# Segment sums of a graph network by products with masks on TensorE instead of running sums on VectorE

## What is computed

```python
h  = relu(layernorm(x))
m  = segment_sum((h * deg_isqrt)[src] * edge_weight[:, None], dst) * deg_isqrt
x1 = x + leaky_relu((h + m) @ W0.T + b0, 0.01)
y  = relu(layernorm(x1))
for l in range(4):                      # edges and one self loop for each node
    p  = y @ W[l]
    al = leaky_relu((p @ a_s)[src] + (p @ a_d)[dst] + ea @ We[l] @ a_e, 0.2)
    al = segment_softmax(al, dst)
    o  = segment_sum(p[src] * al[:, None], dst) + bias[l]
    y  = layernorm(o) * gamma[l] + beta[l]
out = x1 + y
```

## Time and profile before

| | us |
|---|---|
| median of 3 runs | 3035.37 (3034.85 to 3036.59) |
| profiled execution | 3065.14 |
| its span, first to last instruction | 3063.4 |
| busy: PE / PE weight load | 1802.1 / 1333.8 |
| busy: DVE / ACT / POOL | 1893.5 / 1617.7 / 1276.3 |
| mean granted TensorE clock | 0.731 of full |

### The profile page before, as it was taken

How to read it: one execution, slowest core, us unless ns; L and a number is a source line. 1 busy time by engine, 2 the same in 40 slices (tenths; PEclk the granted TensorE clock), 3 DMA queues, 4 the chain that set the end, 5 groups by cost and what they waited for, 6 DMA issues and landing times. The chain is left out here.

```text
span 3063.4 us, 44584 instructions
## 1 busy us (share of the span) xinstructions
PE 1802.1 (59%) x9650; PEld 1333.8 (44%) x9650; DVE 1893.5 (62%) x9080; ACT 1617.7 (53%) x6973; POOL 1276.3 (42%) x989
## 2 busy tenths in 40 slices
PE   1879999950555659598029496049594068592000
PEld 1756666620333436487026385036484045482000
DVE  3069999941888858234878345968246967114970
ACT  0169999940555759233559354559255567233230
POOL 2668787775111257400037500057400067302277
PEclk9998999975555559579559698559697568796555
DMA  3332233310000341000041100131000131003011
GB/s 104 51 78 65 57 86 96 78 29 1 0 0 1 100 113 34 24 1 1 4 124 31 28 1 1 34 97 34 23 1 1 58 75 43 12 1 84 5 35 36
DMA packets 102065, 126.22 MB, mean 41 GB/s; under 512 B 59950, under 2 KB 67945, under 8 KB 98473
## 3 DMA queue, kind: packets, MB, share of 16 engines
q1 hardware_dynamic: 39016, 97.37, 11.2%
q0 software_dynamic: 62400, 25.68, 5.0%
q10 hardware_dynamic: 432, 0.79, 0.1%
HBM read 78.61 MB, written 64.50 MB: 47 GB/s over the span
## 5 line engine op out<-in xcount | busy, mean ns | idle before, releaser
L241 POOL DMA_INDIRECT S<-row_t,INFG x400 | 528.0, 1320 | 1017.9 <-issue 1017.9
L224 PE MATMUL bank<-ident,Y 125*128 125x125 f32 x1000 | 184.7, 316 | 378.1 <-ACT Y L769 234.6
L754 PE MATMUL bank<-AC,XT 128*125 128x384 f32 x800 | 364.0, 565 | 6.7 <-ACT R L817 6.7
L224 PEld LDWEIGHTS bank<-ident,Y 125*128 125x128 f32 x1000 | 135.3, 164 | 491.6 <-DVE Y L908 228.0
L817 ACT ACTIVATE R<-bank 125x128 f32<-125x128 f32 x1200 | 311.2, 274 | 60.6 <-PE bank L754 60.1
L1517 DVE COPY SCS<-bank 125x8 f32 (+1 forms) x100 | 16.7, 167 | 424.7 <-PE bank L1471 424.7
L1491 ACT ACTIVATE XT<-bank,BC,GC 128x500 f32<-128x500 f32 x150 | 114.3, 762 | 287.0 <-PE bank L224 286.8
L817 ACT ACTIVATION_READ_ACCUMULATOR R<-bank 125x1 f32 x1200 | 247.2, 206 | 0.0
L235 PE MATMUL bank<-WC,XT 128*125 128x128 f32 x1600 | 246.4, 301 | 0.0
L235 PEld LDWEIGHTS bank<-WC,XT 128*125 128x125 f32 x1600 | 206.1, 201 | 49.6 <-issue 49.6
L1089 DVE SCALAR_TENSOR_TENSOR R<-R,keep (+1 forms) x496 | 189.7, 413 | 33.5 <-ACT R L1608 29.4
(11 more groups left out here) (263 smaller groups left out, 5035.4 us busy)
## 6 DMA issues: line engine op xcount, KB each, us to landing
R<-in_x SPq DMA_DIRECT2D x100, 224.0 KB
out_rows<-R SPq DMA_DIRECT2D x100, 224.0 KB
row_t<-T SPq DMA_DIRECT2D x20, 1120.0 KB
S<-row_t,INFG POOLq DMA_INDIRECT x400
R<-in_edge_attr SPq DMA_DIRECT2D x1, 5600.0 KB
x_t<-R SPq DMA_DIRECT2D x5, 1120.0 KB
S<-x_t SPq DMA_DIRECT2D x1, 5600.0 KB
R<-in_x SPq DMA_DIRECT2D x100, 26.0 KB
```

Source lines behind the costliest of these rows:

```text
L224: ins = nc.tensor.transpose(ps[:, a * P:(a + 1) * P], t, ident[0:P, 0:P])
L241: pool.indirect_dma_start(to, None, table, bass.IndirectOffsetOnAxis(ap=idx, axis=0), bounds_check=rows - 1, oob_is_err=False).then_inc(do ...
L754: nc.tensor.matmul(LAYERS[HALVES[a]][0:P, 0:3 * D], h0(g, a), AC[:, 0:3, :], start=True, stop=True).then_inc(layers_done.s, 1)
```

## The change

- The edge order in the tiles is turned: edge e lies in tile e // 125, partition e % 125, so that a tile holds 125 neighbouring edges. Scores and softmax weights stay in the other layout (100 partitions x 125 columns, one tile a partition) and are transposed on PE between the two (`columns_in`, `weights_in`).
- A mask `M` of 125 x 125 in bf16 for each tile, 1 where two edges have the same target, is made once (100 broadcasts of the targets' row by PE, 25 comparisons on DVE) and kept in DRAM (`m_t`, 3.1 MB). It is read back into `R` ahead of the convolution and of each attention layer, since `dense` uses `R`.
- The convolution is one loop of 50 units of two `S` and two `T` tiles (`conv_layer`). For each tile DVE multiplies the mask by the edge weights (`mask`), POOL makes a diagonal for the self term, and PE sums source rows with the mask and the target row with the diagonal in one PSUM tile, ahead of the weights. There are no running sums.
- Attention is one block for the softmax and one loop of 50 units: mask product and diagonal product, copy, product with the layer's weights `WCX`, squares, root, rescale; the next layer's source rows are made beside it. Scores for the next layer come out of the same product as columns 128 and 129 (`W` = 130), so rows of `S`, `T` and `row_t` have 520 bytes. The weights are centred as before, and the preceding layer's gamma is multiplied into them.
- A segment that goes from one tile into the next is summed apart: the first and last column of each aggregated tile is kept (`EDGE`), and behind the loop a 101st tile `T[:, 100]` holds these rows, with steps counted by `x_stage`, `x_pe` and `x_act`.
- In the last layer POOL scatters each unit's tiles in the loop (`put`, lag 5), and x1 rows come in pieces of four tiles (`XF`).
- In `dense` the six dot products are columns 384 to 389 of the product for layers 1 to 3; each tile has a PSUM bank of its own, and ACT copies the six columns to `DOT`.
- Setup: indices are made first, the edge attributes are loaded from setup on (to `T`, row by row of 512 bytes).

The core of the diff:

```diff
-                 # dense, PE: layers(a)
-                                pe.wait_ge(*copied2.at(g + 1))
-                                if g >= 2:
-                                    pe.wait_ge(*mixed2.at(g - 1))
-                                for b in range(Q):
-                                    nc.tensor.matmul(DOTS[g % 2][0:P, b, :], h0(g, b), PC[:, :], start=True,
-                                                     stop=True, skip_group_check=True)
-                            nc.tensor.matmul(LAYERS[HALVES[a]][0:P, 0:3 * D], h0(g, a), AC[:, 0:3, :], start=True,
+                            nc.tensor.matmul(LAYERS[a][0:P, 0:3 * D + 6], h0(g, a), ACB[:, 0:3 * D + 6], start=True,
                                              stop=True).then_inc(layers_done.s, 1)
...
+                            nc.scalar.activation(DOT[:, g % NS, :, a], LAYERS[a][0:P, 3 * D:3 * D + 6], ACT.Copy)
...
+                for g in range(EG):          # DVE, masks
+                    dve.wait_ge(s_rowb, g + 1)
+                    nc.vector.tensor_tensor(M[:, g * Q:(g + 1) * Q, :],
+                                            PT[2 + g % 2][0:P, 0:Q * P].rearrange("p (a e) -> p a e", a=Q),
+                                            DS[:, g * Q:(g + 1) * Q].unsqueeze(2).broadcast_to([P, Q, P]),
+                                            ALU.is_equal).then_inc(s_mask, 1)
...
+                    def aggregate(n):        # convolution, PE
+                        pe.wait_ge(*rows1.at(n + 1))
+                        pe.wait_ge(*masked.at(n + 1))
+                        pe.wait_ge(*diag_ready.at(n + 1))
+                        if n >= NS:
+                            pe.wait_ge(*copied2.at(n - NS + 1))
+                        r = n % NS
+                        for a in range(2):
+                            nc.tensor.transpose(PT[r][:, a * P:(a + 1) * P], Y[:, r, a, :], ident[0:P, 0:P])
+                        for a in range(2):
+                            o = PT[r][:, (2 + a) * P:(3 + a) * P]
+                            nc.tensor.matmul(o, Y[:, r, a, :], MA[:, r, a, :], start=True, stop=False,
+                                             skip_group_check=True)
+                            ins = nc.tensor.matmul(o, Y[:, r, 2 + a, :], DGB[:, r, a, :], start=False, stop=True,
+                                                   skip_group_check=True)
+                        ins.then_inc(gathered.s, 1)
...
+                    for t in slots:          # PE, convolution
+                        run_slot(t, NU, [(4, conv), (7, score), (3, aggregate), (6, turn2)])
+                    for t in slots:          # POOL
+                        run_slot(t, NU, [(2, diagonal), (5, residual), (5, add_beta)])
...
+                dma2(sp, R[:, 0:P * C // 2].bitcast(BF16), m_t, s_ml)    # beside the softmax chain
...
+                    def aggregate(n):        # attention, PE
+                        pe.wait_ge(*masked.at(n + 1))
+                        pe.wait_ge(*diag_ready.at(n + 1))
+                        r = n % NS
+                        if n >= NS:
+                            pe.wait_ge(*t_ready.at(n - NS + 1))
+                        for a in range(2):
+                            o = banks[r][:, a * P:(a + 1) * P]
+                            nc.tensor.matmul(o, S[:, 2 * n + a, 0:D], MA[:, r, a, :], start=True, stop=False,
+                                             skip_group_check=True)
+                            ins = nc.tensor.matmul(o, T[:, 2 * n + a, 0:D], DGB[:, r, a, :], start=False, stop=True,
+                                                   skip_group_check=True)
+                        ins.then_inc(gathered.s, 1)
+                    def multiply(bank, xt, copied, done):
+                        def op(n):
+                            r = n % NS
+                            pe.wait_ge(*copied.at(n + 1))
+                            nc.tensor.matmul(product(banks[bank + r], 2 * P), ones3[:, 0:P],
+                                             BR[:, l:l + 1, 0:cols].broadcast_to([3, 2, cols]), start=True, stop=False,
+                                             skip_group_check=True)
+                            for a in range(2):
+                                ins = nc.tensor.matmul(product(banks[bank + r], 2 * P)[:, a, :],
+                                                       XT[:, r, xt + a * P:xt + (a + 1) * P], WCX[:, l, 0:cols],
+                                                       start=False, stop=True, skip_group_check=True)
+                            ins.then_inc(done.s, 1)
+                        return op
+                    for t in slots:          # PE
+                        run_slot(t, NU, [(0, aggregate), (1, multiply_t)] if final else [(0, turn), (0, aggregate), (1, multiply_t), (0, multiply_s)])
+                    for t in slots:          # ACT
+                        run_slot(t, NU, [(3, root), (1, copy_t), (2, squares)])
+                    def mask(n):             # DVE
+                        r = n % NS
+                        if n >= NS:
+                            dve.wait_ge(*gathered.at(n - NS + 1))
+                        nc.vector.tensor_tensor(MA[:, r, :, :], M[:, 2 * n:2 * n + 2, :],
+                                                alphaS[:, 2 * n:2 * n + 2].unsqueeze(2).broadcast_to([P, 2, P]),
+                                                ALU.mult).then_inc(masked.s, 1)
+                    for t in slots:
+                        run_slot(t, NU, [(0, mask), (4, rescale_t), (3, invert), (1, edge)] if final else [(0, mask), (4, rescale_s), (4, rescale_t), (0, copy_s), (3, invert), (1, edge)])
+                    def put(n):              # POOL, last layer
+                        pool.wait_ge(*t_ready.at(n + 1))
+                        for c in (2 * n, 2 * n + 1):
+                            scatter(pool, out, repNI[:, c:c + 1], N, T[:, c, 0:D], s_out)
+                    for t in slots:
+                        run_slot(t, NU, [(0, diagonal)] + ([(5, put)] if final else []))
```

More of the change, by code:

```diff
@@ L35 @@
 C = E // P
+TC = C + 1
+W = D + 2
 Q = 4
 NS = 4
[L38 to L39 removed]
+NU = C // 2
 GROUPS = N // (P * Q)
@@ new lines, in root @@
+                    def root(n):
+                        r, k = n % NS, 2 if final else Q
+                        act.wait_ge(*squared.at(n + 1))
+                        nc.scalar.activation(rt4[:, r, 0:k], ss4[:, r, 0:k], ACT.Sqrt,
+                                             bias=epsc[:, 0:1]).then_inc(rooted.s, 1)
+                    for t in slots:
+                        run_slot(t, NU, [(3, root), (1, copy_t), (2, squares)])
+                    act.wait_ge(*x_pe.at(3))
+                    nc.scalar.activation(YX[:, :], banks[2][0:C, 0:D], ACT.Square, scale=D ** -0.5,
+                                         accum_out=sx[:, 0:1]).then_inc(x_act.s, 1)
```

1335 lines of the change are left out of this document (697 added, 638 removed).

## The result

The changed kernel takes 2477.36 us (median of 4 runs, 2475.16 to 2483.14) against 3035.98 for the kernel before in the same comparison (median of 4 runs, 3034.85 to 3068.20). The ratio on record, over all these runs, is 0.8143 (95% interval 0.8095 to 0.8190); the two medians alone give 0.816. I had forecast 2682, with 2595 as the lower end.

A forecast was written before the change was run, and what follows sets the result against it. No engine bounds the whole: POOL's transfers end the dense stretches, and attention runs in pieces that hardly overlap. 3063.4 + 37 + 24 - 82 - 79 - 79 - 177 = 2707 us span, 2682 as median; range 2595 to 2830.

The forecast's parts named there:

- Convolution: One loop of 50 units at 6.5 us (5.8 with PE at 2.4 GHz, 7.4 at 1.2): 377 us against 353, +24.
- The lock: Convolution: two-input DVE operations wait for POOL's sums on the shared SBUF port; 0.6 us added to DVE's unit.
- Rival 3: PE at 2.4 GHz also in convolution (-25 to -40) and early block (-45): 2606 us as a median; chance 0.13.
- Layer 1's ramp: Start of layer 1's attention loop: 61 us at half clock kept from the earlier trace, costing 25 us.
- Layers: Layers 2 and 3: chain 24, loop 152, ramp 2, tail 9 make 187 us instead of 266, -79 each.
- Last layer: Scatters overlap the loop from slot 5, POOL sets the unit at 3.9 us: 241 us instead of 418, -177.
- Setup and the next block: Ahead of the dense stretch: setup +15, next block with 100 mask broadcasts +20, one more gather +2; sum +37.
- -5 to -20 case: Block with the mask broadcasts: its cost if PE ran them at 2.4 GHz pace, instead of the +20 forecast.
- POOL's cover: Dense stretches: POOL's queue outlasts compute by 87 us in the first, some 20 in a layer, so added work costs nothing.
- Rival 1: PE stays at 1.2 GHz in the new loops: about 3087 us as a median, slower by 1.7%; chance 0.05.
- rival 2: Clock goes up and down in the loops, attention unit 3.6 us, convolution 7: 2818 us as a median; chance 0.15.
- Rival 4: Last layer: scatters wait for the loop, so overlap fails, 379 us there, 2818 as a median; chance 0.04.

The follow-up runs named there:

- conv_slow4: Changed kernel with four more normalisations per unit of the convolution on ACT; convolution stretch 386.6 us against 268.4.
- conv_act_fill: Changed kernel with one more root on ACT and two more score products on PE per convolution unit; convolution stretch 293.8 us against 268.4.
- conv_slow4_fill: Changed kernel with four more normalisations on ACT and eight more score products on PE per convolution unit; convolution stretch 540.4 us against 268.4.
- masks_early: Changed kernel with the masks read back at the end of each dense stretch, not in the block behind it; 2471.5 us (median of 4).
- att_each: Changed kernel, attention units with one more PE transpose (layer 1), DVE copy (2), ACT copy (3); 353.1, 349.3, 348.9 us against 347.9, 348.5, 348.7.
- half_gathers: Changed kernel with every second gather of refreshed source rows left out in the four layers; layers took 319.8, 318.5, 318.3 and 360.4 us.
- conv_act: Changed kernel with one more small root per unit of the convolution on ACT; convolution stretch 304.0 us against 268.4.
- conv_pool: Changed kernel where POOL makes each diagonal of the convolution three times; convolution stretch 305.2 us against 268.4.
- combined: Changed kernel with 60 rather than 50 x gathers in the setup block and masks read at each dense stretch's end; 2444.81 us (median of 5).

## Why the prediction was wrong in size, step by step

- **Convolution (-114 us of the miss).** PE's sum was close: 4.0 us forecast and 3.83 found at full clock, 7.4 and 7.14 at half, though a mask product steps by 0.22 us and not by 0.27. The term that failed is "5.8 us when PE is at 2.4 GHz". In its place the unit is 4.42 us, set by ACT. For DVE I took 5.2 and found 4.15 without the lock: the seven small steps were entered at their recorded durations (near 0.15 each), and cost their engine 0.05 to 0.1 each, 0.5 together; the eight aggregates cost 0.073 each. For ACT I took 4.8 and found 4.42. The lock was 0.6 and is 0.27, and lies in a slack. The second half of the error hangs on the first: "I take 6.5" was a fair value for an engine at 5.8 us a unit (conv_slow4: 6.8 at 5.96), but at 4.42 the clock holds. My ground for it, that the clock goes by PE's duty, doesn't hold in general: 0.87 busy stood at 1.00 (changed kernel), 0.93 busy fell to half four times (conv_act_fill), and a full row stood at 0.52 (conv_slow4_fill). 52.4 x (6.5 - 4.4) = 110 us, and 2 of the rest is the mask load (16 against 18). Rival 3 had this mechanism at 0.13, and put it at 25 to 40 us, since it kept the 5.8.
- **Layer 1's ramp (-23 of -40).** I carried over the 61 us at half clock of the earlier trace rows. After the change layer 1's loop has no such start (0.98, like the others). Why the old loop had one stays open; no run here touches it.
- **Layers (-17 each).** The loop is right: 2.89 us a unit against 2.9, 149.5 us against 154. The exact 2.9 has some luck: the four mask products step 0.98 us with the hand-over behind them, not 1.07, and the first bias with its two products 0.89, not 0.79. From the last gather to the first mask step it is 25 us (1551.5 to 1576.5), where I had 24 for the chain and kept the 13 us between last gather and products of before. But the old products had begun within these 13 us, at 1746, so that 8 were counted twice; the chain is 20 us, not 24. The tail is 7, not 9.
- **Last layer (-31).** The same 12 at its start; 10.7 us to the first scatter, not 14; 185 for the 101 scatters and 44 diagonals, not 191; 5 to the end, not 12. The mechanism is as forecast.
- **Setup and the next block (-22).** +18 us to the first gather, forecast +15; then -5, forecast +20. The masks took 27 us of PE, not 47: they ran at granted clock 1.00 (80.8 to 107 us, recorded from 86 on), and I had priced them at half on the ground that the clock column shows nothing so early. This was my -5 to -20 case, chosen against.
- **Dense stretches (+6).** Held: POOL ends all five. The queue's 8 us aren't shown to be an effect of the change: the same queue took from 586 to 597 us in the other kernels that leave it alone.
- **Mask loads in the layers, ACT's and DVE's share in attention, POOL's cover:** as forecast, shown by masks_early, att_each and half_gathers.
- **From span to median (+27, luck).** I took the median as 0.990 of the traced run, as it was for the kernel before. For the changed kernel it is 1.001 of it. The factor took 27 us off the forecast for no reason in the kernel, and so made the miss smaller.

Rival 1 (half clock throughout) and rival 2 (a clock that goes up and down) fell: convolution and attention ran at 0.98 to 1.00. Both mechanisms lie near, though. 0.20 us more of ACT work a unit brings rival 2's into the convolution (conv_act, 0.83), and 1.54 us more bring it close to rival 1's (conv_slow4, 0.57, with PE busy 50.57 of 51.20 us at half clock). Rival 4 didn't come, and was worth 45 us rather than 138.

## What to carry to other kernels

Price a loop by the distance between starts, not by recorded durations, above all for small steps: an engine that is full may look overbooked on paper. If the engines are within some per cent of each other and PE is one of them, forecast the clock together with the unit: in the changed kernel units of which PE filled 0.87 or more ran at full clock, and a slightly longer one cost 3.6 times the added step. More PE work isn't a cure: a row of PE without a break stood at half clock (conv_slow4_fill). An idle gap of POOL ahead of a stretch that POOL's queue ends is on the path, however busy everything else looks.

## What the runs showed of the hardware that I had not expected

- One more root on ACT (a unit of 4.42 to 4.59 us at full clock) took the granted clock of the convolution from 1.00 to 0.83 and cost 36 us instead of 10; 1.54 us took it to 0.57 and cost 118 instead of 77.
- PE without a break in its busy row can stand at half clock: 150.00 of 150 us at 0.52 in conv_slow4_fill, 50.57 of 51.20 at 0.50 in conv_slow4. What brings the clock down there isn't shown.
- A DVE copy of four columns took 0.23 us instead of 0.13 beside a POOL product that ended within it (conv_pool), although it has one SBUF input. The Trainium skill (SBUF — State Buffer, Who interferes with whom) says that copies can take the port shared with POOL in their two-port modes, an exception that the prediction left out when it named this section; this row agrees.
- POOL's issue of indirect transfers pauses for 2.3 to 4.5 us twice in each full row of 100, in every trace here. A pause that fell into a load of 3.1 MB by SP's queue lasted 7.8 us (masks_early); the same load between two pauses cost POOL nothing (combined).
